# A routed feed-forward kernel: the first schedule read sooner, two copies to a load, and the last plan spread over tiles 8 to 20

## The reference, cut to what matters

```
q, k, v = relu(norm(x) @ Wq + bq), relu(ctx @ Wk + bk), relu(ctx @ Wv + bv)
x = x + relu((relu(q @ k.T) / sqrt(512) + mask) @ v)
z = norm(x); logits = z @ gate_w            # 8 experts
topv, topi = top_k(logits, 2); w = softmax(topv)
Y_e = (silu(z @ Wu_e) * (z @ Wv_e)) @ Wo_e   # for the two chosen experts e
x = x + w[0] * Y_topi[0] + w[1] * Y_topi[1]
```

## Time and profile before

| what | before |
|---|---|
| median of 3 runs | 422.38 us (421.64 to 422.92) |
| the profiled execution | 421.33 us |
| its span, first to last instruction | 419.5 us |
| mean granted TensorE clock | 0.99 |
| DMA | 87.13 MB, mean 208 GB/s |

### The profile page before, as it was taken

One profiled execution on the slowest core, in us unless ns is written; L12 is line 12 of the kernel. 1 busy time (PEld: TensorE's weight loads), 2 busy tenths in 40 slices (PEclk: granted clock), 3 DMA queues, 4 the chain that ended last, 5 costly groups with the idle time before them and its releaser, 6 DMA issues.

```text
span 419.5 us, 10234 instructions
## 1 busy us (share of the span) xinstructions
PE 398.1 (95%) x3031; PEld 356.1 (85%) x3031; DVE 331.8 (79%) x1108; ACT 277.3 (66%) x596; POOL 213.1 (51%) x224
## 2 busy tenths in 40 slices
PE   8999999999999999998989899989999999999990
PEld 5689999999999999997778789889999999999970
DVE  2668899999999999999868888868887666666650
ACT  1677888888889988886677566656676444444420
POOL 2011125656665656564556743323333464888872
PEclk9999999999999999999999999999999999999995
DMA  8821336776766666545795468869965699999793
GB/s 288 276 65 62 102 102 205 249 251 232 246 206 229 213 230 247 179 155 171 250 309 212 181 189 258 275 218 312 293 224 178 200 227 270 311 276 135 97 130 52
DMA packets 49509, 87.13 MB, mean 208 GB/s; under 512 B 7600, under 2 KB 18352, under 8 KB 49328
## 3 DMA queue, kind: packets, MB, share of 16 engines
q1 hardware_dynamic: 35600, 52.37, 39.7%
q0 software_dynamic: 13856, 34.10, 29.2%
HBM read 43.98 MB, written 48.29 MB: 220 GB/s over the span
## 4 chain that ended last, share of the span: by engine, by line
PE 70%; DVE 6%; SPq 6%; issue 5%; ACT 4%; DMA 4%; POOL 2%; POOLq 1%; ACTq 0%
PE psQ L1453 12%; PE psQ L1454 12%; PE psQ L1455 12%; PE psT L1449 11%; PE psO L1453 2%; PE psO L1454 2%; PE psO L1455 2%; PE psZ L1453 2%; SPq L541 2%; PE psZ L1455 2%; PE psZ L1454 2%; PE psS L1453 2%; PE psQ L1449 2%; PE psG L1549 2%; PE psS L1455 2%
## 5 line engine op out<-in xcount | busy, mean ns | idle before, releaser
L900 DVE TENSOR_TENSOR qT<-psT,qT 128x512 fp32r<-128x512 f32 x103 | 69.5, 688 | 29.2 <-ACT qT L708 29.1
L612 POOL DMA_INDIRECT z_dram<-zb x64 | 72.4, 1132 | 31.5 <-DVE zb L1188 16.2
L1453 PE MATMUL psQ<-wuv,qT 128*128 x284 | 86.3, 304 | 0.0
L1454 PE MATMUL psQ<-wuv,qT 128*128 x284 | 80.5, 283 | 0.0
L1455 PE MATMUL psQ<-wuv,qT 128*128 x284 | 80.2, 282 | 0.0
L1453 PE MATMUL psQ<-qT,wq 128*128 128x256 f32 x256 | 75.2, 294 | 1.5 <-DVE qT L900 1.5
L1455 PE MATMUL psQ<-qT,wq 128*128 128x256 f32 x256 | 72.4, 283 | 0.0
L1454 PE MATMUL psQ<-qT,wq 128*128 128x256 f32 x256 | 72.3, 283 | 0.0
L708 ACT ACTIVATE qT<-psT 128x512 fp32r<-128x512 f32 x103 | 59.5, 595 | 15.0 <-PE psT L1449 15.0
L1453 PEld LDWEIGHTS psQ<-wuv,qT 128*128 128x128 f32 x284 | 53.7, 189 | 4.9
L776 ACT ACTIVATE gate_work<-psQ 128x128 f32<-128x128 f32 x71 | 19.6, 277 | 52.8 <-PE psQ L1455 52.8
(11 more groups left out here) (299 smaller groups left out, 1061.3 us busy)
## 6 DMA issues: line engine op xcount, KB each, us to landing
wq_flat<-z_dram SPq DMA_DIRECT2D x28, 264.0 KB, 4.0
xin<-in_x_dram SPq DMA_DIRECT2D x11, 512.0 KB, 3.9
z_dram<-spare SPq DMA_DIRECT2D x17, 264.0 KB, 3.9
qpT_flat<-z_dram SPq DMA_DIRECT2D x11, 264.0 KB, 3.6
zT_ctxT<-in_x_dram SPq DMA_DIRECT2D x5, 512.0 KB, 3.5
kpT_flat<-z_dram SPq DMA_DIRECT2D x9, 264.0 KB, 3.7
vp_flat<-z_dram SPq DMA_DIRECT2D x9, 264.0 KB, 4.5
xn<-z_dram SPq DMA_DIRECT2D x8, 264.0 KB, 3.7
```

The lines of the kernel that those rows point to most:

```text
L612: pool.indirect_dma_start(out=z_dram, out_offset=bass.IndirectOffsetOnAxis(ap=z_of(b)[:, t, ROW_COL + k:ROW_COL + k + 1].bitcast(U32), axi ...
L900: nc.vector.tensor_tensor(o, a, b, ALU.subtract).then_inc(s, 1)
L1453: pe.matmul(o, w[LO], a[HI], start=first, stop=False)
L1454: pe.matmul(o, w[HI], a[LO], start=False, stop=False)
```

## The change

It has four parts.

1. **First schedule.** In block 14 the steps plan_ends(0) and plan_rows(0) go ahead of keep_stats. turn_sched(0) waits for `s_relu` of block 14 (ACT has read the score bank) in place of `lg_ready`. keep_sched(0) on DVE goes ahead of choose.all() and logits_low in the last block, while plan_used(0) stays.
2. **First tiles.** On ACT gate(1) and gate(2) go ahead of the two halves of turned_z(14). On PE gates(14) moves from before tile_body(2) into it, behind down(1).
3. **Copies.** Two copy_tail stand behind each of the loads 17 to 20, and none behind 21 to 24.
4. **Last plan.** plan_lengths(1) moves from tile 7 to tile 8, and all later steps move by one tile or more; know_pads moves from tile 7 to tile 11, behind keep_sched(1). lists_skips and lists_rows share tile 17. turn_sched(1) and (2) stand in tiles 11 and 20.

```diff
@@ SP
-                if EARLY <= t < EARLY + E:
+                if EARLY <= t < EARLY + E // 2:
                     if t == EARLY:
                         sp.wait_ge(pads_known, 2)
                         sp.wait_ge(head_stored, 16 * E)
-                    copy_tail(t - EARLY)
+                    for e in range(2):
+                        copy_tail(2 * (t - EARLY) + e)
@@ ACT
+            gate(1)
             turned_z(last + (-1), 0, psS)
-            gate(1)
             turned_g(3)
             turned_s(1)
+            gate(2)
             turned_z(last + (-1), 1, psS)
             again(0)
             norm2(last, 0)
             gate_logits(last + (-1))
-            gate(2)
@@ DVE, body
                 if prv.real:
                     masked(prv)
+                if b.n == EARLY_NB + 3:
+                    keep_sched(0)
                 if third.real:
                     choose.all()
                 if prv.real:
                     logits_low(prv)
                 if b.n == EARLY_NB + 3:
                     plan_used(0)
-                    keep_sched(0)
...
-                if prv.real:
-                    keep_stats(prv)
                 if ends_early:
                     plan_ends(0)
                     plan_rows(0)
+                if prv.real:
+                    keep_stats(prv)
@@ DVE, tiles
                     Weigh(last).all()
+                if t == 8:
                     dve.wait_ge(place, PLACE_STEPS * NB)
+                    plan_lengths(1)
+                if t == 9:
+                    plan_ends(1)
+                if t == 10:
+                    plan_rows(1)
+                if t == 11:
+                    keep_sched(1)
                     know_pads()
-                    plan_lengths(1)
-                if t == 8:
-                    plan_ends(1)
-                if t == 9:
-                    plan_rows(1)
-                if t == 10:
-                    keep_sched(1)
+                if t == 12:
                     plan_used(1)
...
-                if t == 19:
+                if t == 20:
                     keep_sched(2)
-                if t == 20:
+                if t == 21:
                     keep_kinds()
@@ PE
                 if g == 0:
-                    pe.wait_ge(lg_ready, NB - 1)
+                    pe.wait_ge(s_relu, NB - 1)
...
                     down(t - 1, expert_of(t - 1))
                     del expert[t - 1]
+                if t == 2:
+                    gates(Step(NB - 2))
...
-                if t == 10:
+                if t == 11:
                     turn_sched(1)
-                if t == 19:
+                if t == 20:
                     turn_sched(2)
...
             turn_z(last + (-1), 1, psS)
-            gates(last + (-1))
             tile_body(2)
```

More of the change, by code:

```diff
@@ L1409, in _ @@
                     Weigh(last).all()
+                if t == 8:
                     dve.wait_ge(place, PLACE_STEPS * NB)
-                    know_pads()
-                    plan_lengths(1)
-                if t == 8:
-                    plan_ends(1)
-                if t == 9:
-                    plan_rows(1)
-                if t == 10:
-                    keep_sched(1)
+                    plan_lengths(1)
[5 more added lines that the diff above has]
+                    keep_sched(1)
+                    know_pads()
+                if t == 12:
                     plan_used(1)
-                if t == 11:
+                if t == 13:
                     lists_sizes()
-                if t == 12:
+                if t == 14:
                     lists_rests()
-                if t == 13:
+                if t == 15:
                     lists_ends(range(0, 3))
-                if t == 14:
+                if t == 16:
                     lists_ends(range(3, 5))
                     lists_starts()
-                if t == 15:
+                if t == 17:
                     lists_skips()
-                if t == 16:
                     lists_rows()
-                if t == 17:
+                if t == 18:
                     lists_heads()
-                if t == 18:
+                if t == 19:
                     lists_cuts()
-                if t == 19:
+                if t == 20:
                     keep_sched(2)
-                if t == 20:
+                if t == 21:
                     keep_kinds()
```

## The result

The changed kernel took 424.22 us (median of 8 runs, 423.51 to 424.76), the kernel before 422.19 us beside it (8 runs, 421.12 to 424.07). The ratio is 1.0041, with a 95% interval of 1.0022 to 1.006: slower by 1 to 2.5 us. The forecast was 427.9 us with a range of 425.2 to 430.5. In two of the five comparisons of the experiments the kernel before took 422 us as here, in the other three 431 to 434 us, so each ratio is against the kernel before of its own comparison; three executions, of two kernels, that took 999 us are in no number.

The account below looks back on a forecast made before the run. PE, busy 95% of the span, was taken as the bound. Tile 25 coming 5.3 us later plus 0.2 for slow spells gave 421.33 + 5.5 = 426.8 us profiled; 1.05 more gave a median of 427.9, range 425.2 to 430.5.

Parts of the forecast that it names:

- SP's time for two copies: SP's queue, loads 17 to 20: a second copy costs 1.92 us, a step becomes 5.0 us; turn_g(25) 5.3 us later.
- turn_sched(0)'s 1.6 us: PE's wait at the first schedule: goes, but comes back as a wait for logits_low before attend(14); net 0.
- the arrival of load 21: SP's queue: load 21 issued at 269.4, landing 4.3 us later at 273.7; PE would come at about 266.0.
- rival C: Tile 25: load 25 is late as well, PE waits 1.5 us there, 429.4 us in all; chance 10%.
- slow spells: SP's queue ahead of load 21: one slow spell may fall there, 0.2 us added, making +5.5 us.
- A: Tile loads keep their lead and the gain is real: turn_g(25) 1.3 us sooner, 421.1 us; chance 3%.
- the limit of 0.6: SP's queue: a copy may cost no more than 0.6 us for turn_g(25) to come no later than before.
- B: First schedule: its 1.5 us is kept and the whole tile phase moves by it, 426.4 us; chance 5%.
- D: PE's clock falls to 1.2 GHz in the load waits; one or two tiles take 2.7 us more, about 431.5; chance 6%.

Follow-up runs that it names:

- part 3 alone: Kernel before with two copies behind each of loads 17 to 20, nothing else changed: 1.0072 beside 422.25 us; elsewhere 1.0024, 1.0073 and 1.01.
- all but part 3: Changed kernel with one copy behind each of loads 17 to 24: 1.0046 of the kernel before beside 422.25 us; elsewhere 1.0086, 1.0106 and 1.0091.
- the kernel with constant rows: Changed kernel with its eight copies at fixed addresses, no register reads, some tiles wrong: 0.9966 of the kernel before beside 431.62 us, 0.9916 beside 422.41.
- copies on POOL a tile sooner: Changed kernel with copies issued by POOL behind stores 10 to 17, not 11 to 18: 0.9933 of the kernel before beside 422.25 us; elsewhere 0.9997 and 1.0014.

## Why the prediction was right and wrong

**Right.** What decides is SP's time for two copies, and the waits are at tiles 19, 20 and 21, three times, as named. Schedule 1 was ready at 246.25 (246.6 forecast), gated(8) let turn_s(8) go at 235.84 (gated(8) was forecast near 235.6), and turn_sched(0)'s 1.6 us moved to lgT. From turn_g(21) to tile 25 PE needed 11.18 us (11.2). That the reads on SP are what costs was shown by taking them away.

**Wrong, in the trace.** The step that failed is the arrival of load 21, its landing above all: "It is issued at 260.03 + 1.65 + 4 x 1.92 = 269.4 and lands 4.3 us later, at 273.7." It was issued at 268.50 and landed 3.0 us later. The 0.9 us of the issue are schedule 1 (0.35) and SP's way from it to load 21 (0.5). On that way the second copies cost a little more than written, 1.93 to 2.16 us where 1.92 stood, 0.5 us in all. But the forecast had built on the measured start of load 21, and in that lay two slow steps of 3.9 to 4.0 us, from load 17 to 19, which came back only in part. The larger part, 1.3 us, is the landing, for which the forecast took the middle of the old stretch and allowed no less than 3.2. In the three profiles of two copies to a load beside 422 us, the two of the changed kernel and one of part 3 alone, load 21 landed in 3.0 to 3.3 us. Why so soon stays open. That the change leaves the DMA engines freer explains little: from 249 to 270 us they moved 239 GB/s against 250 before, since each of the rarer loads now brings two copies along. With load 21 sooner the three waits came out at 1.6 to 1.8 us, where 3.2, 2.3 and 2.3 were written. The Trainium skill's figure ("DMA: Bandwidth & Descriptors", section on the anatomy of one DMA), by which the forecast estimated 2.6 us, lay below every tile load issued from 244 to 275 us in the traces beside 422 us (3.0 to 6.4), though nearer to this one than 4.3 was. The other way went load 25, 0.44 us late, a third of rival C: its schedule came at 277.4, and it took 4.83 us to land, beyond the 2.9 to 4.3 allowed. With the 0.2 us that the forecast had added for slow spells, -0.9 - 1.3 - 0.2 + 0.44 are, but for rounding, the 1.9 us between the forecast's +5.5 and the +3.6 at turn_g(25); the end gives back another 0.3.

**Wrong, in the sum.** "The median lies 1.05 us above the profiled execution, so the median to expect is 427.9." The changed kernel's profiled execution lay 0.39 above its median, so this term was 1.4 us too high, as large as the landing: the second step that failed. The two traces differ by 3.3 us of span, the medians by 2.0. The runs of before reach over 3.0 us, those of the changed kernel beside it over 1.25, and profiled executions from the two ends of such ranges overstate the difference.

**Left out, in where it comes from.** The forecast counted the later schedule as 1.65 us ahead of load 21 and called part 3 the step that decides. It did not ask what that schedule does where part 3 is undone. By its own rows the eighth copy then holds load 25 by as much, and all but part 3 costs 0.2 to 0.7% alone. The sum was not harmed, because the two don't add, but whoever had undone part 3 alone would have kept a loss.

**Rivals.** A (a gain) was out once a copy cost SP 1.9 to 2.2 us where it had to cost under 0.6; the kernel with constant rows, at about 0.9, did gain, for there all eight copies became cheaper and not only the four added ahead of load 21, which the limit of 0.6 was worked out for. B did not happen. C happened by a third. D was half right: the clock stays at its upper level in one profile of the changed kernel and falls to the lower in another, at a price of 1.75 us where 2.7 was written. The Trainium skill ("TensorE: Matmul & The Clock Gate", section on HAM oscillation) says that a DMA wait between groups of matmuls can bring this about; the traces agree that it can, not that it must: behind waits of 1.8, 2.2 and 2.6 us the clock fell, behind three of 1.6 to 1.8 us and one of 2.3 and one of 2.8 us (load 25, with one copy to a load) it stayed at 1.00, so the length of the wait alone doesn't decide it.

## What to carry to other kernels

Where one queue issues everything that a bottleneck engine waits for, count its instructions and not its bytes: a copy addressed from registers cost this queue 1.9 us or more, over two thirds of the 2.67 us that PE needs for a tile, and a neighbour engine took all eight at no cost that the runs beside 422 us show. Where a sum hangs on one load, a landing time from the middle of a stretch is no more than a guess: here the stretch had 3.2 to 5.1 us before and 3.0 to 4.2 after, and the load that decided had the shortest. Before you put a loss on one part of a change, ask what the other parts do at the same event: of two delays that meet in one wait only the later one counts, and undoing it alone brings the other out. And a single profiled execution carries up to 3 us of its own here; a forecast of 1% needs the place of that execution among the runs on both sides.

## What the runs showed of the hardware

A DRAM-to-DRAM copy with both rows read from memory into registers cost SP 1.9 to 2.2 us from issue to issue, with constant rows about 0.9 us. On POOL the same copy is 0.56 us of busy time behind 0.5 to 1.2 us of its own sequencing. The kernel before took 9 to 12 us more in three of five comparisons, and every kernel that ran in both kinds of comparison was 8 to 15 us slower there. The mean granted clock of these runs reaches lower (0.974 to 0.991, against 0.982 to 0.992). In the pair of traces set side by side, the time is lost in tiles 0 to 10, in short waits and in spells at the lower clock; from turn_g(13) on the distance stays at 12.7 to 13.0 us. Here the windows of one and the same kernel, copies on POOL a tile sooner, over the same stretch, first where the kernel before took 422 us and then where it took 431:

```profile
238.00:246.00 8.00, 7.98 (x59) 6.79 (x57) 7.08 (x24) 5.10 (x11) 6.17 (x7) 1.00 0.55 216
```

```profile
238.00:246.00 8.00, 6.11 (x32) 5.47 (x33) 4.86 (x18) 4.27 (x10) 4.62 (x5) 0.79 0.36 136
```

Both stand on the same chip at different times, so the cause is not a slow chip; what it is stays open, and no kernel was run to find it.
